# The second values product of a group, moved from the end of its step to the beginning, in two softmax attentions

## What is computed

```python
qkv = (x @ Wqkv).reshape(b, l, 3, H, HD)
attn = softmax(einsum('bhqd,bhkd->bhqk', q, k) * HD ** (-0.5), axis=-1)
out = einsum('bhqk,bhkd->bhqd', attn, v)
```

## Time and profile before

| | |
|---|---|
| median of three runs | 2075.91 us (2070.33 to 2081.99) |
| the profiled execution | 2072.57 us, its span 2070.8 us |
| PE busy in the span | 1601.6 us, 77% |
| ACT busy in the span | 842.2 us, 41% |
| L1236, values | 2048 records, 177.2 us, mean 421 ns |
| L1364, exponentials | 256, 262.2 us, mean 1024 ns |
| mean granted clock of PE | 0.874 |

### The profile page before, as it was taken

How to read it: one execution, slowest core, us unless ns; L and a number is a source line. 1 busy time by engine, 2 the same in 40 slices (tenths; PEclk the granted TensorE clock), 3 DMA queues, 4 the chain that set the end, 5 groups by cost and what they waited for, 6 DMA issues and landing times. The chain is left out here.

```text
span 2070.8 us, 47042 instructions
## 1 busy us (share of the span) xinstructions
PE 1601.6 (77%) x16785; PEld 1171.0 (57%) x16785; DVE 1141.1 (55%) x3082; ACT 842.2 (41%) x1602; POOL 555.0 (27%) x774
## 2 busy tenths in 40 slices
PE   2779799999488879699977677988986587343882
PEld 1646566666255647488864454555554587333882
DVE  4655577777434447355544576866774343642334
ACT  1422355555211115344422354655552576002661
POOL 3111011111101103433202211132333355364551
PEclk9989899999799989899988896988896799556996
DMA  4000222221099970000001002222220242211224
GB/s 167 1 1 1 64 61 53 60 55 43 21 176 180 178 120 1 1 4 3 3 2 63 1 1 64 67 66 62 66 63 21 65 109 81 88 51 45 74 73 139
DMA packets 148169, 123.98 MB, mean 60 GB/s; under 512 B 17040, under 2 KB 135696, under 8 KB 147312
## 3 DMA queue, kind: packets, MB, share of 16 engines
q1 hardware_dynamic: 139312, 103.30, 23.6%
q0 software_dynamic: 8640, 17.78, 2.6%
HBM read 32.73 MB, written 54.60 MB: 42 GB/s over the span
## 5 line engine op out<-in xcount | busy, mean ns | idle before, releaser
L1437 DVE TENSOR_REDUCE small<-ps 128x8 f32<-128x1024 f32 (+1 forms) x256 | 312.7, 1224 | 127.1 <-PE ps L1223 70.8
L1364 ACT ACTIVATE scr<-ps 128x1024 f32<-128x1024 f32 x256 | 262.2, 1024 | 245.9 <-PE ps L1198 121.1
L243 POOL TENSOR_TENSOR rstd<-vare,neghalf 128x4 f32<-128x4 f32 (+1 forms) x80 | 71.4, 892 | 580.6 <-DVE vare L222 580.2
L1236 PE MATMUL ps<-scr 128*32 128x256 f32 x2048 | 177.2, 421 | 0.2 <-ACT scr L1364 0.2
L2761 POOL DMA_INDIRECT results<-scr x142 | 136.1, 958 | 152.5 <-DVE scr L2750 66.5
L1185 PEld LDWEIGHTS ps<-scr_r 32*128 32x128 f32 x1024 | 83.8, 199 | 155.8 <-ACT scr L1364 84.9
L1185 PE MATMUL ps<-scr_r 32*128 32x256 f32 x1024 | 138.6, 350 | 33.2 <-ACT scr L1364 19.5
L2682 PE MATMUL ps<-scr 128*128 128x128 f32 x1136 | 155.1, 281 | 3.9 <-issue 2.3
L1216 PE MATMUL ps<-scr_r 32*128 32x256 f32 x1024 | 140.1, 356 | 9.9 <-DMA scr_r<-scr_r 5.4
L2682 PEld LDWEIGHTS ps<-scr 128*128 128x128 f32 x1136 | 142.4, 197 | 5.8 <-issue 5.7
L2743 DVE TENSOR_TENSOR scr<-ps,scr 128x256 f32<-128x256 f32 x142 | 60.3, 425 | 142.3 <-ACT scr L2728 106.3
(11 more groups left out here) (403 smaller groups left out, 3521.8 us busy)
## 6 DMA issues: line engine op xcount, KB each, us to landing
scr_r<-scr_r SPq DMA_DIRECT2D x512, 64.0 KB
rows_m<-logits SPq DMA_DIRECT2D x8, 2064.0 KB, 31.3
rows_f<-logits SPq DMA_DIRECT2D x8, 2064.0 KB, 31.2
scr<-results SPq DMA_DIRECT2D x32, 256.0 KB
scr<-rows_m SPq DMA_DIRECT2D x71, 64.5 KB
scr<-rows_f SPq DMA_DIRECT2D x71, 64.5 KB
scr<-in_l3m SPq DMA_DIRECT2D x1, 3072.0 KB, 10.9
results<-scr POOLq DMA_INDIRECT x142
```

The costliest lines, as they stand in the source:

```text
L243: pool.tensor_tensor(k.rstd[:, 0:self.J], k.vare[:, 0:self.J], k.neghalf[:, 0:self.J], ALU.pow).then_inc(self.e["rstd_ready"].sem, 1)
L1236: ins = pe.matmul(ps[32 * r:32 * r + 32, 6, col:col + 256], Vp[:, c % 2, 4 * kt + r, at:at + 32], PT[:, g % 2, r, kt * 256:kt * 256 + 256] ...
L1364: act.activation(PT[:, g % 2, 2 * x:2 * x + 2, :], ps[:, 4:6, :], ACT.Exp).then_inc(e["prob_ready"].sem, 1)
L1437: dve.tensor_reduce(nf[:, half, 0:blocks, at:at + 2].rearrange("p q a -> p a q"), ps[:, 2 * (p % 2):2 * (p % 2) + 2, :].rearrange("p a (q ...
```

## The change

In an odd step the values block (kt = 1) is issued before the step's scores. In an even step it stays where it was. Which block belongs to which step stays the same.

```diff
         for b, s in steps:
             c, p = nat_of(b, s)
+
+            late_values = (b, s // 2 - 1, s % 2) if s > 1 else (b - 1, 3, s)
+            if s % 2 and has(late_values[0]):
+                values(*late_values)
             for turn in range(5):
                 if has(b):
                     turned_scores(b, s, turn)
@@ -1344,8 +1348,8 @@
-            if has(b if s > 1 else b - 1):
-                values(*((b, s // 2 - 1, s % 2) if s > 1 else (b - 1, 3, s)))
+            if s % 2 == 0 and has(late_values[0]):
+                values(*late_values)
```

## The result

The changed kernel takes 2111.6 us (median of four runs, 2103.85 to 2119.63), the kernel before 2074.55 beside it. The ratio is 1.0194, with a 95% interval from 1.0146 to 1.0242. The forecast was 2113.

A forecast was written before the change was run, and what follows sets the result against it. Each step was taken as bound by the larger of a serial PE-ACT floor and PE's work up to its values block's end. First attention +20.4 and second +17 gave +37 us on 2075.91, so 2113 us, range 2098 to 2124.

The forecast's parts named there:

- The price of the second block: Values blocks in even steps: a second block directly behind the first adds 0.44 us; 0.57 is the upper bound.
- (a): Rival: the second block costs the full 0.57 us in both attentions, total about 2126 us; chance 0.12.
- First attention, one batch: Steps 0 to 7 of one batch: even steps grow, odd ones fall towards the floor, sum +1.36 us.
- First attention, all: Whole first attention: fourteen batches give 19.0 us, the first and last together 1.4, sum +20.4 us.
- Second attention: Whole second attention: +1.35 us a batch over 16 batches, 21.6, with corrections +17 us, bounds about +5 and +28.
- the line of three corrections: Second attention: -3.4 us for step 7 in odd batches, -3.1 for seven late exponentials, +2 for the lower clock.
- the clock's term: Second attention: at 1.2 GHz a second block adds between 0.44 and 1.01 us; put at +2 us.
- the -0.57 of step 7 in the odd batches: Second attention, odd batches 3 to 13: step 7, with the sort's matmuls, loses a 0.57 us block; six times, -3.4.
- (b): Rival: more time at the lower clock, PE's idle time being gathered in odd steps; total 2139 us; chance 0.10.
- (c): Rival: second blocks fill part of seven stalls, second attention's clock rises to 0.94, 28 us return; 2085 us; chance 0.12.
- (d): Rival: PE's total work decides, not the loop; 126 pairs save 0.13 us each, 16 us; 2060 us; chance 0.06.
- (e): Rival: the change does nothing, since the waits order the work anyway; 2076 us; chance 0.04.

The follow-up runs named there:

- first_only: The change in the first (causal) attention alone, against the kernel before: ratio 1.0097, 20.45 us a batch.
- pair_in_odd: Kernel before with both values blocks of a group at the end of the odd step, none in the even step: ratio 1.0041, 19.47 us a batch.
- fill_both: Kernel before with step 2's values ahead of turn_maxima and step 6's block moved to step 7's end (not in sort batches): ratio 0.9932, 2010.76 us.
- before_again: The kernel before, unedited, run again on the next chip: ratio 1.0004, second attention 308.7 us.
- after_again: The changed kernel, unedited, run again on the next chip, against the kernel before: ratio 1.0204, second attention 325.3 us.
- second_only: The change in the second attention alone, against the kernel before: ratio 1.0153, second attention 321.4 us.
- split_six: Changed kernel with step 6's first block ahead of the housekeeping and the second behind it: step 6 takes 3.17 us, the one execution 2134.81 us.
- after_fill_two: Changed kernel with step 2's first block ahead of turn_maxima: ratio 1.0101 against the kernel before, second attention 297.1 us.

## Why the prediction was right, point by point

- **Which bound.** Right. The time follows the loop, step by step, and not PE's total: `first_only`, `pair_in_odd` and `fill_both` do the same work on PE and give 20.45, 19.47 and 18.49 us a batch.
- **The price of the second block.** 0.44 from one row at the end of the first attention; step 6 grew by 0.45 (2.45 to 2.90). Rival (a) is out.
- **First attention, one batch.** +1.36 forecast, +1.40 measured. Step 0 +0.26, steps 1 and 2 together +0.43, step 3 -0.01, step 4 +0.40, step 5 -0.12, step 6 +0.45, step 7 -0.01. The small gains in steps 3 and 7 are not there: the floor behind these steps is 2.22 and not 2.18.
- **First attention, all.** +20.4 forecast, +27.6 in the trace. Six of the 7 us are the last batch, in which the clock fell: 22.2 us from its first to its last exponential in place of 15.4, of which 0.7 was forecast. I had said that the clock would hold at 0.97; it was 0.96. In that batch there are no natural scores to fill PE's odd steps: PE stands idle for 1.11 us behind those of step 1.
- **Second attention.** +17 forecast, +15.2 in the traces beside the result, and +16.6 between those of `before_again` and `after_again`. The size came out right by two errors that cancel. The steps' own share is about 18, as the sum without its correction for late signals had it (21.6 - 3.4 = 18.2, +2 for the clock). But the clock was worth some 21 us in the trace of `second_only`, about 14 by its medians, and not 2, where nothing else disturbs. And the seven late exponentials did not merely hide a block each: all seven were gone (the one late exponential of the changed kernel stands elsewhere, in step 3 of the last batch), and with them the stretches at 1.2 GHz that had followed. The step that failed is the line of three corrections: the clock's term was too small by seven to ten times, and the late signals were taken as fixed in place. A smaller error: the -0.57 of step 7 in the odd batches is real (2.70 to 2.12), but in step 0 behind it L263 waits for DVE's places, so that this step grows by 0.57 and not by the 0.18 of an undisturbed batch. The term should have been about -1 and not -3.4. Nor does the lower bound follow from its terms: 2 x 0.44 x 16 - 3.4 - 3.1 is +7.6 and not +5.
- **The total.** 2113 forecast, 2111.6 measured, and part of it is luck. In the traces the two attentions grew by 43 us and not by 37, and the whole by 47; the median lies 8 us below the profiled execution.
- **The rivals.** (b) happened in part: the clock did cost, in the last batch of the first attention and in the second, there mostly behind the wait in step 2 and not for the idle time of the odd steps, as (b) had argued. (c) happened too, in another form than priced: not by filling the stalls, but by their absence. (d) and (e) are excluded by `first_only`. The Trainium skill, "TensorEngine Tiling (Array Packing)", Key Properties, says that a change of tiling mode drains TensorE; `split_six` (0.28 us for two more changes) and the pair (0.13 us less) agree, and it was too small to decide. The Trainium skill, "TensorE: Matmul & The Clock Gate", Part 1, says that the array is slow by default and that activity releases it; `after_fill_two` agrees, with a mean clock of 0.94 in place of 0.84.

What stays open: what delays PE's signals beside the result and on one of the three chips and not on the other two, and why they are rarer when the values stand elsewhere. It was seen in traces alone. Which signal it is can be read: in the traces of before it is the one of the scores (L1191), which arrives 1.6 to 2.1 us after their end, while the values' signal, for which the exponential of step 6 waits too, has come over 2 us earlier.

## What to carry to other kernels

Where a loop through a second engine has one buffer, each step costs the larger of two times, and work that is moved from a step with cover to one without it costs its full length, however much is saved elsewhere: sum the steps one by one. A step that gets shorter wins nothing if the next one waits for a chain that started in it. Put loose work into such a wait; that was worth 0.7 to 0.8% here, and the clock of the second attention was 0.95 and 0.98 in place of 0.92.

## What the runs showed of the hardware

- Two blocks of four column tiles in a row hold the next instruction for 1.01 us, one for 0.57, at 2.4 GHz; at 1.2 GHz 1.86 and 1.01.
- With idle stretches of 1.2 to 1.3 us in front of L1287 in step 2 the granted clock of the second attention had a mean of 0.83 to 0.84 over 324 to 331 us, so 104 to 113 us of it at 1.2 GHz; with a block of 0.57 in that stretch it was 0.94 over 300, so 36 us.
- The same program differs by up to 4% between chips (2012.96 to 2087.78 us); of the 77 us between the traces of before on these two, 26 lie in the second attention and the rest outside both attentions. In the two traces of before with the longer times six and seven exponentials of the second attention start 1.6 to 2.1 us after the end of the matmuls that release them, with up to 2.95 us of idle time ahead of them; in the one with the shorter time, and where the second attention is unedited in `first_only`, none does:

```profile
1412.75 1.02 ACT L1364 ACTIVATE scr<-ps 128x1024 f32<-128x1024 f32 x1 [2.88 <-remote]
```
